# Attention A's first heads stacked on chip by selection matmuls, and its row maxima taken one and a half halves ahead of the scores instead of two

## The reference

```
q = h @ wq + bq ; k = h @ wk + bk ; v = h @ wv + bv     # h: 1024 x 512, layernormed
32 query heads of 16, 8 groups of keys and values, 4 query heads to a group
scores = q . k * 16**-0.5 ; probs = softmax(scores) ; out = probs @ v ; x + out @ wo + bo
```

## Time and profile before

| | us |
|---|---|
| median of 3 runs | 1570.75 (1566.34 to 1572.21) |
| the profiled execution, its own time | 1571.05 |
| its span, first to last instruction | 1569.2 |
| TensorE busy | 1469.0 (94%) |
| VectorE busy | 1237.7 (79%) |
| ScalarE busy | 868.9 (55%) |
| GpSimd busy | 237.6 (15%) |

### The profile page before, as it was taken

How to read it: one execution, slowest core, us unless ns; L and a number is a source line. 1 busy time by engine, 2 the same in 40 slices (tenths; PEclk the granted TensorE clock), 3 DMA queues, 4 the chain that set the end, 5 groups by cost and what they waited for, 6 DMA issues and landing times.

```text
span 1569.2 us, 23528 instructions
## 1 busy us (share of the span) xinstructions
PE 1469.0 (94%) x7932; PEld 698.8 (45%) x7932; DVE 1237.7 (79%) x2583; ACT 868.9 (55%) x1468; POOL 237.6 (15%) x174
## 2 busy tenths in 40 slices
PE   5779999999999997899999999998999999999988
PEld 3412333333333354455555555554555555555534
DVE  4288888888886388787897887887887888878873
ACT  2205767676778324565665665664665665646630
POOL 2002000000000132221212212212212212211020
PEclk9957999999999998999999999999999999999989
DMA  3894000000000233566576575675684674653621
GB/s 97 150 143 134 1 1 0 0 0 0 0 0 11 64 94 98 105 140 144 121 137 139 120 150 127 129 147 120 128 160 111 141 145 110 134 96 67 115 54 54
DMA packets 352234, 144.64 MB, mean 92 GB/s; under 512 B 314680, under 2 KB 324408, under 8 KB 352128
## 3 DMA queue, kind: packets, MB, share of 16 engines
q1 hardware_dynamic: 352144, 143.48, 43.8%
HBM read 59.64 MB, written 6.19 MB: 42 GB/s over the span
## 4 chain that ended last, share of the span: by engine, by line
PE 73%; DVE 14%; ACT 6%; DMA 3%; issue 3%; SPq 0%; POOL 0%; DVEq 0%; ACTq 0%
PE ps L1433 9%; PE ps L1215 9%; PE ps L1435 9%; PE ps L1434 9%; PE ps L1268 7%; PE ps L1254 7%; PE ps L1395 4%; PE ps L1514 3%; PE ps L1516 3%; PE ps L1515 3%; ACT hl L680 2%; DVE hl L1038 2%; PE ps L1358 2%; DMA scratch<-pieces 2%; PE ps L1458 2%
## 5 line engine op out<-in xcount | busy, mean ns | idle before, releaser
L672 ACT ACTIVATE x<-ps,nmb,factor 128x128 f32<-128x128 f32 (+7 forms) x256 | 211.6, 832 | 290.9 <-DVE nmb L1023 290.9
L823 DVE TENSOR_REDUCE mx<-ps 128x1 f32<-128x512 f32 x512 | 326.4, 686 | 52.8 <-PE ps L1215 49.4
L581 ACT ACTIVATE proj<-ps 128x1024 f32<-128x1024 f32 x256 | 248.4, 1021 | 105.7 <-PE ps L1254 104.8
L1215 PE MATMUL ps<-ks,qs 96*128 (+1 forms) x512 | 200.1, 414 | 16.3 <-DVE mx L823 8.5
L1038 DVE SCALAR_TENSOR_TENSOR hl<-x,rden,hl 128x128 f16<-128x128 f32 (+7 forms) x256 | 208.3, 814 | 4.6 <-ACT hl L680 4.3
L680 ACT ACTIVATE hl<-x,rden 128x128 f16<-128x128 f32 (+7 forms) x256 | 184.1, 767 | 23.2 <-DVE rden L1034 22.5
L1021 DVE TENSOR_REDUCE nmr<-ps 128x1 f32<-128x128 f32 (+7 forms) x256 | 191.9, 750 | 0.0
L500 POOL TENSOR_TENSOR tmp<-tmp 128x640 f32<-128x640 f32 x64 | 98.4, 1538 | 532.1 <-DVE tmp L1017 532.1
L1433 PE MATMUL ps<-wh,xTh 128*128 128x256 f16 (+1 forms) x512 | 167.6, 327 | 0.0
L1434 PE MATMUL ps<-wl,xTh 128*128 128x256 f16 (+1 forms) x512 | 167.5, 327 | 0.0
L1435 PE MATMUL ps<-wh,xTl 128*128 128x256 f16 (+1 forms) x512 | 167.4, 327 | 0.0
(11 more groups left out here) (155 smaller groups left out, 2149.6 us busy)
## 6 DMA issues: line engine op xcount, KB each, us to landing
scale<-sp_n SPq DMA_DIRECT2D x32, 384.0 KB, 4.3
st<-in_L_attn_b_qw_q_dram SPq DMA_DIRECT2D x32, 256.0 KB, 2.8
st<-in_L_attn_b_qw_o_dram SPq DMA_DIRECT2D x32, 256.0 KB, 3.0
scale<-so_n SPq DMA_DIRECT2D x32, 256.0 KB, 3.6
qs<-scratch SPq DMA_DIRECT2D x24, 256.0 KB, 8.4
hlT<-hl SPq DMA_TRANSPOSE x256, 3.5
scratch<-pieces SPq DMA_DIRECT2D x5, 768.0 KB, 13.4
xnat<-attn_a_hidden_state_dram SPq DMA_DIRECT2D x8, 256.0 KB, 4.8
```

The source lines that it names most:

```text
L581: nc.scalar.activation(pbuf[:, e % 4, :].rearrange("p (b n) -> p b n", b=2), ps[:, b:b + 2, :], ACT.Exp, scale=float(HD) ** -0.5).then_inc ...
L672: nc.scalar.activation(pr[:, h, 0:n], flat(2 * (h % 2), n), ACT.Exp, bias=nmb[:, h:h + 1], scale=factor[:, par, 0:1], accum_out=den[:, h:h ...
L823: nc.vector.tensor_reduce(mx[:, f, k // 2, k % 2:k % 2 + 1], ps[:, bank(k), :], AX.X, ALU.max).then_inc(s_mx, 1)
L1215: mm(ps[:, bank, :], qs[0:STACK, ds(g * R + h, 1), f * HALF + qt * P:f * HALF + (qt + 1) * P], ks[0:STACK, ds(g, 1), kh * HALF:(kh + 1) * ...
```

## The change

- **Order on GpSimd.** The memset of the three rows of `ks` moves from the beginning to behind the layernorm. In its place GpSimd builds five selection matrices (`sel`, in the space of `x`): one clear and twelve small copies of `identb`.
- **Stacking on chip.** For key group 0 and the first four query heads TensorE multiplies the three parts by a selection matrix (`select`, six matmuls of 512 columns for each of five stacks), which puts the six part rows into 96 PSUM rows. ScalarE copies four of the stacks and VectorE one into `ks` and `qs`. The DRAM path goes on for the rest: seven of eight key heads, four of eight of the first query tile, all of the others.
- **Order on TensorE.** Two projections, `select(0)`, half of the third projection, `select(1)` and `(2)`, then the 32 maxima of half 0 with the other `select`s and 16 of the remaining projection matmuls between them; both `rows`; 16 maxima of half 1 with the last projection matmuls and the value projection between them; the first scores; only then the wait for the DRAM stacks.
- **Splits of the last three tiles.** Both remainders move from VectorE to GpSimd.
- **Lag.** The prologue does 48 maxima instead of 64. Half u does the second 16 of half u + 1 and the first 16 of half u + 2. Half 14, which had none, does 16. `negate` moves from the start of the half to behind the first 16; `rows` move from steps 3 and 4 to 5 and 6, `row_copy` with them.
- **Last group.** Weight blocks 0 and 1 stand at the end of half 14, 2 and 3 at steps 0 and 1 of half 15, 4 to 6 at its steps 4 to 6 (before: 0 to 2 at steps 5 to 7 of half 14, 3 at step 0, 4 to 6 at steps 3 to 5 of half 15).

```diff
-ROWS_AT = (13, 18)
+ROWS_AT = (21, 26)
+AHEAD = MM + MM // 2
 def max_at(k):
-    return k + (k >= 4) + (k >= 12) + (k >= 16)
+    return k + (k >= 4) + (k >= 20) + (k >= 24)
...
# SP queue
+                    h0 = {4: 1, 0: R}.get(j, 0)
+                    dst, part = (ks[rows, h0:], K_PART[b]) if j == 4 else (qs[rows, 8 * j + h0:8 * j + 8, :], Q_PART[b])
+                    sp.dma_start(dst, scratch[n, part, h0 * HD:].rearrange("(h d) n -> d h n", d=HD)).then_inc(s_stk[j], 16)
...
# GpSimd
-            pool.memset(ks[STACK:STACK + NEG], 1.0).then_inc(s_set, 1)
+            pool.memset(sel, 0.0).then_inc(s_set, 1)
+            pool.wait_ge(s_idb, 1)
+            for b in range(len(K_PART)):
+                rows = slice(HD * b, HD * b + HD)
+                pool.tensor_copy(sel[:, 0, K_PART[b], rows], identb[:, 0:HD]).then_inc(s_set, 1)
+                pool.tensor_copy(sel[:, 1:5, Q_PART[b], rows],
+                                 identb[:, 0:R * HD].rearrange("p (h d) -> p h d", h=R)).then_inc(s_set, 1)
+            pool.wait_ge(s_xh, T)
+            pool.memset(ks[STACK:STACK + NEG], 1.0).then_inc(s_set, 1)
             for n in range(5):
+                if n >= 2:
+                    pool.wait_ge(s_q32, 2 * n + 2)
+                    pool.wait_ge(s_p3, n)
+                    pool.tensor_tensor(r32, q32, parts[:, n % 2, 0, :], ALU.subtract).then_inc(s_r1, 1)
                 pool.wait_ge(s_r1, n + 1)
                 pool.tensor_copy(parts[:, n % 2, 1, :], r32).then_inc(s_p2, 1)
+                if n >= 2:
+                    pool.wait_ge(s_p2, n + 1)
+                    pool.tensor_tensor(parts[:, n % 2, 2, :], r32, parts[:, n % 2, 1, :], ALU.subtract).then_inc(s_p3, 1)
...
# ScalarE
+            q_high(0, 4)
+            q_high(1, 0)
+            stacked(0)
+            stacked(1)
+            stacked(3)
+            stacked(4)
+            q_high(2, 1)
+            q_high(3, 2)
...
             for r in range(2):
                 row_copy((0, 0), r, 2)
+            q_high(4, 3)
             exps(0, False, True)
...
# VectorE, a half
                     if not (last and f == 1):
+                        ahead(0, 4)
...
                     if f == 1:
                         normalise(g, 0)
...
                     if not (last and f == 1):
+                        ahead(4, MM // 2)
+                        negate(u + 1, 1 - f)
                     if not last:
+                        ahead(MM // 2, MM)
...
# TensorE, prologue
+            for n in range(2):
                 for c in range(2):
                     for k in range(KC):
+                        project_a(n, c, k)
+            select(0)
+            for k in range(KC):
+                project_a(2, 0, k)
+            select(1)
+            select(2)
...
             for k in range(MM):
...
+                if k >= RING:
+                    pe.wait_ge(s_mx, k - RING + 1)
+                maximum(0, 0, k, k % RING)
+                if k == 3:
+                    select(3)
+                elif k == 7:
+                    select(4)
+                if k % 2 and k < 8:
+                    project_a(2, 1, k // 2)
+                elif k % 2 and k < 24:
+                    project_a(3, (k - 8) // 8, k // 2 % 4)
+                elif k % 2:
+                    project_a(4, 0, k // 2 % 4)
...
+            for k in range(MM // 2):
                 pe.wait_ge(s_mx, MM + k - 2)
+                if k == 1:
                     pe.wait_ge(s_rw, 2)
+                maximum(0, 1, k, (k + 1) % RING)
+                if k % 2 and k < 8:
+                    project_a(4, 1, k // 2)
+                elif k >= 8:
+                    values_a(k - 8)
...
             for r in range(2):
                 scores(0, 0, 0, r, True)
+            pe.wait_ge(s_stk[4], 16 * len(K_PART))
+            pe.wait_ge(s_stk[0], 16 * len(K_PART))
             group_a(0, False, True)
```

195 lines of the change are left out of this document (122 added, 73 removed).

## The result

The changed kernel takes **1555.17 us** (median of 6 runs, 1549.65 to 1559.76) against 1570.55 (6 runs, 1566.34 to 1572.21) for the kernel before on the same chip. The ratio is 0.9901 (95% interval 0.9876 to 0.9926): 15.4 us less. The forecast was 1541 with a range up to 1554, so the direction is right, the time lies 1.2 us above the range, and half of the forecast gain of 29.3 us is missing. The profiled executions are 1559.76 (span 1558.0, clock 0.982) and 1571.05: 11.3 us apart.

What follows compares the result with a forecast made beforehand. VectorE's maxima at half clock bound the prologue, TensorE's order of work a steady half. -30.7 + 3.3 - 3.4 - 3 + 4 + 0.5 = -29.3 us from 1571.05 gave 1541.8, 1541 on the median, range 1530 to 1554.

Steps and rivals of the forecast that it cites:

- part 9: Half 1 of attention A: GpSimd's additions may lie over the negation; +0.5 us (0 to 1.2).
- part 7: 13 steady halves: negation and normalise apart, reduction at the turn can go; -3 us (+8 to -9).
- part 6: First half of attention A: TensorE comes to it from dense work, less cold clock; -3.4 us (0 to -4).
- Part 1: Layernorm: with the memset moved, the last statistics end at 8.0, 1.8 us earlier, and the whole chain with them.
- Parts 2 to 5: Prologue to the first score: first score at 94.7 instead of 125.43, -30.7 us, and +3.3 for two costs.
- Item (a): Clock falling in the pause between the two sets of maxima, slowing the 16 with values; 2 us (0 to 15).
- Item (b): First negation in the prologue: its small casts may wait for GpSimd's last subtraction; 1.3 us (0 to 2.5).
- Part 8: Last group: half 14 gets 16 maxima, copies of the weight blocks come late; +4 us (2 to 7).
- The rivals: Besides the two below: steady halves gain and clock holds, about 1532, chance 0.13; DRAM stacks still gate, 1566 to 1571, 0.02.
- The one at 1557: Prologue: the clock stays low through the 16 maxima with values, 15 us more instead of 2; 1557, chance 0.10.
- The slower rival: Steady halves: TensorE waits for negation, transposes and copies in a row, 4.1 us a half; 1597, chance 0.03.
- the four signs of being wrong: Clock of 0.50 after 79; cast of some us at 74; turn distance over 25.4; TensorE waiting for `qs<-scratch` anywhere.

Runs made afterwards that it cites:

- new lag alone: Kernel before with its old prologue, memset and DRAM stacks, but the new order of the halves, 48 maxima ahead and the new last group: 1566.12 us, ratio 0.9996.
- memset alone: Kernel before with only the memset of the three rows of ks moved behind the layernorm: 1566.53 us, ratio 0.9992.
- before, negation cut: Kernel before with the negation cut from five steps to three (second and third part of the maximum left out): 1560.56 us, one run.
- before, fillers: Kernel before with eight matmuls whose result nobody reads at each group start of attention B: 1574.71 us, ratio 1.0031.
- after again: The changed kernel as it is, run and profiled a second time: 1554.81 us, ratio 0.9901 to the kernel before.
- additions late: Changed kernel with GpSimd's eight additions of bo to x moved from the first group behind the last group's value copy: 1548.40 us, ratio 0.9852.
- values in the pause: Changed kernel with five of eight value projections moved into TensorE's wait for the negation and row copies: 1553.97 us, ratio 0.9905.
- after, negation cut: Changed kernel with the negation cut from five steps to three (second and third part of the maximum left out): 1543.17 us, one run.
- subtraction waits: Changed kernel with GpSimd's last subtraction of the fourth tile held until VectorE's first negation is done: 1553.23 us, one run.
- after, fillers: Changed kernel with eight matmuls whose result nobody reads at each group start of attention B: 1544.28 us, ratio 0.983.
- all mended: Changed kernel with late additions, value projections in the pause, filler matmuls, the waiting subtraction and VectorE's second value addition directly behind its first: 1534.99 us, ratio 0.979.

## Why the prediction was wrong, point by point

By the two profiled executions the gain is 18.0 us short of the forecast (11.3 for 29.3): 9.1 behind attention A, which had no term; 4.7 between the first two turns (part 9); 3.75 in the eleven halves (part 7); 0.9 in the first half (part 6); and 0.4 better up to the first score.

The first output matmul of attention A and all that follows it, in the profiled executions of all kernels:

| kernel | attention A | behind it | group ends that fell |
|---|---|---|---|
| before | 524.22 | 1046.8 | 0 |
| new lag alone | 518.52 | 1046.0 | 0 |
| memset alone | 520.56 | 1049.4 | 2 |
| before, negation cut | 514.33 | 1046.2 | 0 |
| before, fillers | 521.38 | 1054.8 | 1 (and a wait at all seven) |
| after | 503.87 | 1055.9 | 5 |
| after again | 502.67 | 1054.5 | 3 |
| additions late | 496.22 | 1054.2 | 4 |
| values in the pause | 500.53 | 1055.9 | 5 |
| after, negation cut | 489.29 | 1053.9 | 3 |
| subtraction waits | 497.60 | 1055.6 | 5 |
| after, fillers | 497.83 | 1046.5 | 0 |
| all mended | 489.20 | 1045.9 | 0 |

**The step that is missing** is the largest: the sum ended at attention A. It took for granted that what stands behind moves as a block, and never named it. The six profiles with the short prologue and no fillers take 1053.9 to 1055.9 there; with fillers it is 1045.9 and 1046.5. That is about 8 us. The group ends account for 5.2 to 9.3 us of it in each. The rows were there to be read: the same table of group ends for the kernel before shows TensorE standing for 1.02 and 0.69 us at six of seven, and the prologue had shown that a clock can fall in a pause. The prediction weighed the clock for the prologue alone. What makes the falls frequent after the short prologue and rare after the old one is **not shown**. The code there is the same; what differs is when it runs, and the falls move between executions of one kernel. In every profile the ends that fell are neighbours (3 to 7, 1 to 3, 4 to 7, 2 to 4 and so on), so their number is no count of separate events. What can be said is that such a series began in six of six profiles with the short prologue and in one of four with the old one, fillers left aside. The Trainium skill, page "TensorE: Matmul & The Clock Gate", section "What's actually happening", says that the number of matmuls that run at the low clock before it rises at a kernel's start differs between runs of one kernel. The traces agree for the start: in the same code the granted clock from 17 to 31 us is 0.63 in the second profile of the changed kernel and 0.88 in the run with late additions, and the first reduction starts at 49.2 and 46.6. No run here shows what decides it, there or at the group ends.

**Part 9 was mis-sized by a factor of ten:** +0.5 with an upper bound of 1.2, measured +4.95 (4.9 by the run with late additions; 5.6 and 1.9 in two other executions). The mechanism had been named and was right, and the place too. The bound was that of one wait: one addition of 1.24. But the negation is five steps that depend on one another, each short beside an addition, and GpSimd has the next addition going before VectorE issues the next step. Each step pays: 0.3 + 3 x 1.0 = 3.3 us. `rows` then come 3.3 us late, TensorE idles in a half that has no slack, and the clock falls to 0.93 over 25 us for the rest.

**Part 7 had the wrong sign:** -3 forecast, +1.0 over the eleven halves from the second turn to the thirteenth (0.09 a half). It lay inside the bounds (+8 to -9), which is why it costs 4 us and no more. Two arguments failed. That negation and `normalise` no longer stand together is true and worth nothing: the negation's time is on the path in either place (0.43 and 0.40 us for two steps of 0.2). The reduction of 0.69 at the turn did leave the chain there, but it had stood on it because of the negation ahead of it; with the negation the stall moved to the `rows`. The other stall of a half, 3 us ahead of the turn, was in no row of the prediction and stayed.

**Part 1, the memset:** right. -1.87 alone. In the profile of after it is -0.92, since its last input tile arrived later (its last statistics start at 8.26), a difference of arrival and not of the edit.

**Parts 2 to 5, up to the first score:** right, -27.8 for -27.4, and for most of the reasons given. That it fits to 0.4 is luck: the same code reached the first score at 95.81 in the second profile (-29.6) and at 94.9 and 94.6 in two runs whose edits come later. First reduction 49.4 for 48.7. The first 32 maxima end at 72.4 (73.8), with TensorE and VectorE both busy. Item (a), the clock of part 5, is real: 0.67 and 0.72 from 73 to 90; filling the pause moved the first score by 5.9 us (4.1 against the second profile), more than the 2 that were taken for the clock, though part of it is TensorE's idle time that the values now use. Item (b) measured 1.84 at the cast, for 1.3 with a bound of 2.5; the rule that gave the full subtraction was the better guide.

**Part 6:** -2.5 for -3.4. The difference is less than executions differ by: up to the first turn the same code of the kernel before took 32.07 us in one and 29.89 in another. No engine waited for the DRAM stacks, as the prediction said.

**Part 8:** right, +4.1 for +4, and by the mechanism named: TensorE waits for VectorE's late copies of the weight blocks.

```profile
485.48 0.66 PE L1317 MATMUL ps<-ident,xT 128*128 128x128 f32 x4 [0.57 <-DVE fw L877]
```

**The rivals.** None came. The one at 1557 has nearly the measured time for a wrong reason: the clock was back at 1.00 from 90 on, ahead of the first score. It would have been easy to take it for the explanation; the distances between turns and the 1055.9 us behind attention A tell them apart. The slower rival (4.1 us a half) was far off, at 0.1.

**The signs.** Three of the four signs of being wrong came: the low clock after 79, the cast of some us (2.02 at 72.66), and a turn distance over 25.4 (25.46). They named the right places; two of them (the clock and the cast) had been paid for in the sum.

**The range.** It took in the bounds of each named step by itself (the 15 us of (a) lead to 1554, the +8 of part 7 to 1552), not two of them together, and part 9 went over its own bound. What it lacked most was width for what it didn't name: 8 us from code that the change doesn't touch.

## What to carry to other kernels

When work is moved beside another engine's train of instructions, count the waits by the number of small dependent steps that meet it, not once. Sum up to the last instruction of the kernel, not of the stage that is changed: look in the trace of before for places further on that are only just free of a stall (pauses of TensorE that repeat at each turn of a loop), and give them a term of their own. And when a gain is half of what was worked out, compare distances between events that both kernels have, stage by stage, before thinking of a reason; and profile the same kernel twice, since what moves between the two is not a property of the edit.

## What the runs showed of the chip that was not expected

- The granted clock fell after pauses that add up to 1.70 us (1.02 and 0.69) at some group ends and held at others with the same pauses, in one execution. The ends that fell were neighbours in each. A fall cost about 1.6 us (17.05 and 17.10 against 15.43), a wait for the transfer without one 0.6 (16.05). Eight matmuls of 512 columns whose result nobody reads removed all falls in the one kernel (8.0 to 9.4 us behind attention A), and cost 5 us in the other, whose profile had none.
- The start of one and the same code differed by 3 us between executions (first reduction at 46.4 to 46.8 or at 49.0 to 49.4).
- A small VectorE step of 0.2 us took 1.20 beside GpSimd's additions of 1.24, three times in a row; a cast took 2.02 beside a subtraction of 2.12. Reductions from PSUM beside the same additions kept their 0.69.
- GpSimd's subtraction of 128x1024 took 2.12 us and its cast of that size 1.04, against the 2.5 that was worked out from the smaller additions and the 1.0 that was taken for the cast.
